# Self-attention on one Trainium2 core: for some query tiles the row maximum is taken from a key-half difference, rectified on ScalarE, with one VectorE pass

## What is computed

```
qkv = h @ w_qkv + b_qkv
q, k, v = jnp.split(qkv, 3, axis=-1)          # 16 heads of 16 features
scores = jnp.einsum('bqhd,bkhd->bhqk', q, k) / np.sqrt(DK)
attn = jax.nn.softmax(scores, axis=-1)
o = jnp.einsum('bhqk,bkhd->bqhd', attn, v)
```

## Time and profile before

| What | Value |
|---|---|
| median of three runs | 2838.29 us |
| profiled execution, first to last instruction (its span) | 2841.2 us |
| projection stage, first bias operation to the first value addition | 616.2 to 660.7 us |
| value tiles, to the next stage | 660.7 to 674.4 us |
| first passes of pairs 0 and 1, alone | 682.6 to 729.2 us, granted clock 0.50 |
| loop with interleaved first pass, 14 pairs | 729.3 to 1134 us, granted clock 1.00 from 758 us on |
| last two pairs | 1134 to 1174 us |
| reductions of the first pass (L1762) | 512, of 682 ns each on the mean |
| exponentials (L1740) | 256, of 1021 ns |

### The profile page before, as it was taken

One profiled execution on the slowest core, in us unless ns is written; L12 is line 12 of the kernel. 1 busy time (PEld: TensorE's weight loads), 2 busy tenths in 40 slices (PEclk: granted clock), 3 DMA queues, 4 the chain that ended last, 5 costly groups with the idle time before them and its releaser, 6 DMA issues. The chain is left out here.

```text
span 2841.2 us, 39450 instructions
## 1 busy us (share of the span) xinstructions
PE 2161.8 (76%) x11928; PEld 1566.3 (55%) x11929; DVE 1271.6 (45%) x2848; ACT 819.6 (29%) x1698; POOL 438.1 (15%) x362
## 2 busy tenths in 40 slices
PE   5587988836899999722999953599999984794298
PEld 4346674622222222321899943488888884584297
DVE  3874672186877777222323343222222222673222
ACT  1120342110355555400333320133333331341021
POOL 0000000000000000005122200444444441000312
PEclk8698998977799999955999965699999997896599
DMA  2001210013001010063122216222222222007121
GB/s 94 32 1 41 66 57 27 4 52 84 23 24 35 24 35 13 13 232 105 32 32 35 31 37 238 71 55 48 50 55 50 49 39 65 3 1 266 52 33 27
DMA packets 128952, 158.27 MB, mean 56 GB/s; under 512 B 24266, under 2 KB 108499, under 8 KB 128693
## 3 DMA queue, kind: packets, MB, share of 16 engines
q1 hardware_dynamic: 100661, 123.14, 14.2%
q0 software_dynamic: 28032, 32.60, 6.6%
HBM read 110.32 MB, written 57.24 MB: 59 GB/s over the span
## 5 line engine op out<-in xcount | busy, mean ns | idle before, releaser
L1377 PE MATMUL banks<-m_rowsT,x_normT 128*128 128x128 f32 x4032 | 491.9, 282 | 51.3 <-DVE m_rowsT L1439 39.1
L1377 PEld LDWEIGHTS banks<-m_rowsT,x_normT 128*128 128x128 f32 x4032 | 474.6, 196 | 87.4 <-issue 79.2
L1387 PE MATMUL banks<-e_w,m_hT 128*128 x2016 | 456.3, 379 | 2.5 <-ACT m_y L1472 2.5
L1387 PEld LDWEIGHTS banks<-e_w,m_hT 128*128 128x128 f32 x2016 | 373.2, 190 | 49.2 <-issue 3.7
L1462 ACT ACTIVATE m_hT<-banks,m_bias 128x128 f32<-128x128 f32 x848 | 241.7, 368 | 414.7 <-PE banks L1377 414.7
L1762 DVE TENSOR_REDUCE sh_mhalf<-banks 128x1 f32<-128x512 f32 x512 | 318.6, 682 | 76.3 <-PE banks L1665 71.7
L1740 ACT ACTIVATE sh_pT<-banks 128x1024 f32<-128x1024 f32 x256 | 249.5, 1021 | 210.5 <-PE banks L1718 210.4
L1334 POOL DMA_INDIRECT scratch_acc<-m_y,m_ids x106 | 181.6, 1713 | 536.5 <-ACT m_y L1472 368.3
L1443 DVE COPY m_ids<-m_rows 128x1 int32<-128x1 int32 x126 | 19.3, 153 | 527.9 <-POOLq L1340 527.9
L1665 PE MATMUL banks<-sh_ks,sh_qs 96*128 96x512 bf16 x512 | 196.1, 416 | 53.6 <-DVE sh_mhalf L1762 33.2
L1424 DVE TENSOR_SCALAR x_normT<-e_w 128x2048 f32 x129 | 160.9, 1248 | 152.7 <-PEq L1393 92.6
(11 more groups left out here) (310 smaller groups left out, 2516.8 us busy)
## 6 DMA issues: line engine op xcount, KB each, us to landing
e_w<-L_W SPq DMA_DIRECT2D x32, 1024.0 KB, 12.9
m_rows<-scratch_rows SPq DMA_DIRECT2D x126, 132.5 KB, 2.2
e_w<-L1f_W SPq DMA_DIRECT2D x16, 1024.0 KB, 12.0
a_bt<-bias SPq DMA_DIRECT2D x16, 616.0 KB, 4.0
scratch_parts<-sp_part SPq DMA_DIRECT2D x48, 128.0 KB, 1.9
sh_qs<-scratch_parts SPq DMA_DIRECT2D x96, 64.0 KB, 2.7
sh_ks<-scratch_parts SPq DMA_DIRECT2D x96, 64.0 KB, 2.8
scratch_acc<-x_resid SPq DMA_DIRECT2D x2, 2048.0 KB, 9.1
```

Source lines behind the costliest of these rows:

```text
L1377: mm = pe.matmul(ps[:, H_BANK + f // 4, f % 4 * P:(f % 4 + 1) * P], w1_tile[:, u, k, f * P:(f + 1) * P], rowsT[:, u, k, :], start=(k == 0) ...
L1387: mm = pe.matmul(ps[:, Y_BANK, 0:D], hT[:, u, f, :], w2_sb[:, bass.ds(e, 1), f, :], start=(f == 0), stop=(f == FB - 1))
```

## The change

For a tile in the new form the maximum over both key halves is computed as the maximum over columns of max(s0, s1) = s1 + relu(s0 - s1). The projection stage computes differences of the key halves, splits them into three bf16 parts, and stores them to a new tensor `scratch_key_steps`. The stack load gets a third kind of transfer (`kd`). In such a tile the first product (bank 0) uses `kd` and gives the difference; ScalarE rectifies it into `rise`; the second product (bank 1) gives the scores of the second half; and VectorE adds `rise` and takes the row maximum with one `tensor_tensor_reduce`. Tiles 1, 4, 7, 9, 12 and 15 of pairs 2 to 15 have this form, and all 16 tiles of pairs 0 and 1. The maxima are now split behind the transpose, so `turn_maxima` has one transpose, `join_maxima` one operation and `maxima_rows` four. The turn of pair 0's maxima is moved behind four chunks of pair 1.

```diff
+RISING_PAIRS = (1, 4, 7, 9, 12, 15)
...
+                    if j >= 2 and c % 2:
+                        m = (n - NQ // 2) // 2
+                        sp.wait_ge(d_split, m + 1)
+                        for i in range(PARTS):
+                            sp.dma_start(parts_d[i, (j % 2) * P:(j % 2 + 1) * P, c // 2 * CH:(c // 2 + 1) * CH], part_d[i][:, m % 2, :]).then_inc(d_stored[m % 2], 16)
...
+                    sp.wait_ge(d_stored[u], 2 * 48)
...
                     if n >= 2:
...
+                    if n > NQ // 2 and n % 2 == 0:
+                        act.wait_ge(d_taken, (n - NQ // 2) // 2)
...
+                    if n >= NQ // 2 and u:
+                        m = (n - NQ // 2) // 2
+                        v = m % 2
+                        dve.tensor_tensor(d32[:], q32[:, 0, :], q32[:, 1, :], ALU.subtract).then_inc(d_taken, 1)
+                        dve.wait_ge(d_taken, m + 1)
+                        if m >= 2:
+                            dve.wait_ge(d_stored[v], 48)
+                        link(dve.tensor_copy(part_d[0][:, v, :], d32[:]))
+                        link(dve.tensor_tensor(d32[:], d32[:], part_d[0][:, v, :], ALU.subtract))
+                        link(dve.tensor_copy(part_d[1][:, v, :], d32[:]))
+                        dve.tensor_tensor(part_d[2][:, v, :], d32[:], part_d[1][:, v, :], ALU.subtract).then_inc(d_split, 1)
...
+            for s in range(NP):
+                for pair in range(2 * KT):
...
                     for j, (i, k) in enumerate(PROD):
+                        sp.dma_start(kd[u][j * DK:(j + 1) * DK, :, :], steps(k)).then_inc(stack_in[u], 16)
...
-                    pe.wait_ge(stack_in[u], 16 * 2 * len(PROD) * (s // U + 1))
+                    pe.wait_ge(stack_in[u], 16 * 3 * len(PROD) * (s // U + 1))
                 if n >= 2:
-                    pe.wait_ge(a_max, n - 1)
-                pe.matmul(ps[:, A_BANK + n % 2, :], qs[u][0:SR, h, t * P:(t + 1) * P], ks[u][0:SR, h, half * CH:(half + 1) * CH],
-                          start=True, stop=True).then_inc(a_mm, 1)
+                    if half == 0 and (c - 2) % NA // 2 in RISING[(n - 2) // NA]:
+                        pe.wait_ge(a_rise, rise_count[n - 1])
+                    else:
+                        pe.wait_ge(a_max, max_count[n - 1])
+                keys = kd[u][:, h, :] if half == 0 and c // 2 in RISING[s] else ks[u][0:SR, h, half * CH:(half + 1) * CH]
+                pe.matmul(ps[:, A_BANK + n % 2, :], qs[u][0:SR, h, t * P:(t + 1) * P], keys, start=True, stop=True).then_inc(a_mm, 1)
...
-                    for i in range(PARTS):
-                        mm = pe.transpose(ps[0:2 * KT, T_BANK, i * P:(i + 1) * P], mpart[i][:], core.ident[:])
-                    mm.then_inc(mT_mm, 1)
+                    pe.transpose(ps[0:2 * KT, T_BANK, 0:P], m32[:], core.ident[:]).then_inc(mT_mm, 1)
...
                 for c in range(NA):
                     first_pass(pe, 0, c)
+                for c in range(4):
+                    first_pass(pe, 1, c)
...
-                for c in range(NA):
+                for c in range(4, NA):
                     first_pass(pe, 1, c)
...
+                def rises(s, pair):
+                    if pair not in RISING[s]:
+                        return
+                    n = s * NA + 2 * pair
+                    i = rise_count[n]
+                    act.wait_ge(a_mm, n + 1)
+                    if i >= 2:
+                        act.wait_ge(a_max, max_at[i - 2])
+                    act.activation(rise[:, i % 2, :], ps[:, A_BANK, :], ACT.Relu).then_inc(a_rise, 1)
...
+                for s in range(2):
+                    for pair in range(2 * KT):
+                        rises(s, pair)
...
+                        if s + 2 < NP:
+                            rises(s + 2, n % (2 * KT))
                         act.wait_ge(b_mm, n + 1)
...
-                        dve.wait_ge(a_mm, n + 1)
-                        dve.tensor_reduce(mhalf[:, half, h * KT + t:h * KT + t + 1], ps[:, A_BANK + n % 2, :], AX, ALU.max).then_inc(a_max, 1)
-                def split_maxima(s):
-                    dve.wait_ge(a_max, (s + 1) * NA)
-                    link(dve.tensor_tensor(m32[:], mhalf[:, 0, :], mhalf[:, 1, :], ALU.max))
-                    link(dve.tensor_scalar(m32[:], m32[:], -1.0, None, ALU.mult))
-                    link(dve.tensor_copy(mbf[0][:], m32[:]))
-                    link(dve.tensor_copy(mpart[0][:], mbf[0][:]))
-                    link(dve.tensor_tensor(m32[:], m32[:], mpart[0][:], ALU.subtract))
-                    link(dve.tensor_copy(mbf[1][:], m32[:]))
-                    link(dve.tensor_copy(mpart[1][:], mbf[1][:]))
-                    dve.tensor_tensor(mpart[2][:], m32[:], mpart[1][:], ALU.subtract).then_inc(m_split, 1)
...
+                        if c // 2 not in RISING[s]:
+                            dve.wait_ge(a_mm, n + 1)
+                            dve.tensor_reduce(mhalf[:, s % 2, half, col:col + 1], ps[:, A_BANK + half, :], AX, ALU.max).then_inc(a_max, 1)
+                        elif half:
+                            dve.wait_ge(a_mm, n + 1)
+                            dve.wait_ge(a_rise, rise_count[n])
+                            dve.tensor_tensor_reduce(larger[:], ps[:, A_BANK + 1, :], rise[:, (rise_count[n] - 1) % 2, :], 1.0, -3e38,
+                                                     ALU.add, ALU.max, mhalf[:, s % 2, 0, col:col + 1]).then_inc(a_max, 1)
...
+                    dve.wait_ge(a_max, max_count[(s + 1) * NA])
+                    dve.tensor_tensor(m32[:], mhalf[:, s % 2, 0, :], mhalf[:, s % 2, 1, :], ALU.max).then_inc(m_split, 1)
...
                 def maxima_rows(s):
...
-                    dve.tensor_copy(mT[:], ps[0:2 * KT, T_BANK, 0:PARTS * P].rearrange("p (i n) -> p i n", n=P)).then_inc(mT_sb, 1)
+                    top = ps[0:2 * KT, T_BANK, 0:P]
+                    link(dve.tensor_scalar(mT[:, 0, :], top, -1.0, None, ALU.mult))
+                    link(dve.scalar_tensor_tensor(mrest[:], top, -1.0, mT[:, 0, :], ALU.mult, ALU.subtract))
+                    link(dve.tensor_copy(mT[:, 1, :], mrest[:]))
+                    dve.tensor_tensor(mT[:, 2, :], mrest[:], mT[:, 1, :], ALU.subtract).then_inc(mT_sb, 1)
...
+                link(dve.memset(mhalf[:], -3e38))
...
-                split_maxima(0)
+                join_maxima(0)
+                reduce_scores(1, range(0, 6))
...
-                reduce_scores(1, range(NA))
-                split_maxima(1)
+                reduce_scores(1, range(6, NA))
+                join_maxima(1)
...
                         reduce_scores(s + 2, range(12, NA))
-                        split_maxima(s + 2)
+                        join_maxima(s + 2)
...
```

More of the change, by code:

```diff
@@ L1610, in self_attention @@
             ks = [sb3(f"ks{u}", [SR + PARTS, 2, SEQ], BF16) for u in range(U)]
[L1611 to L1614 removed]
+            kd = [sb3(f"kd{u}", [SR, 2, CH], BF16) for u in range(U)]
+            rise, larger = sb3("rise", [P, 2, CH]), sb3("larger", [P, CH])
+            mhalf, m32 = sb3("mhalf", [P, 2, 2, 2 * KT]), sb3("m32", [P, 2 * KT])
+            mT, mrest = sb3("mT", [2 * KT, PARTS, P], BF16), sb3("mrest", [2 * KT, P])
             pT = sb3("pT", [P, 4, 2, CH])
@@ L1623, in self_attention @@
             NA = 2 * KT * 2
+            RISING = tuple(RISING_PAIRS if s >= 2 else range(2 * KT) for s in range(NP))
+            rise_count, max_count = [0], [0]
+            for s in range(NP):
+                for pair in range(2 * KT):
+                    rising = pair in RISING[s]
+                    rise_count += [rise_count[-1] + rising] * 2
+                    max_count += [max_count[-1] + (not rising), max_count[-1] + (not rising) + 1]
             @block.sync
@@ L1734, in _ @@
             def _(act):
+                def rises(s, pair):
[7 more added lines that the diff above has]
+                    act.activation(rise[:, i % 2, :], ps[:, A_BANK, :], ACT.Relu).then_inc(a_rise, 1)
+                max_at = [max_count[s * NA + 2 * pair + 2] for s in range(NP) for pair in range(2 * KT) if pair in RISING[s]]
+                for s in range(2):
+                    for pair in range(2 * KT):
+                        rises(s, pair)
                 for s in range(NP):
                     for n in range(s * 2 * KT, (s + 1) * 2 * KT):
+                        if s + 2 < NP:
+                            rises(s + 2, n % (2 * KT))
                         act.wait_ge(b_mm, n + 1)
```

12 lines of the change are left out of this document (8 added, 4 removed).

## The result

The changed kernel takes 2855.74 us (median of 4 runs, 2850.61 to 2858.44), the kernel before 2837.09 us beside it (4 runs, 2834.23 to 2839.83). The ratio is **1.0053, 95% interval 1.0036 to 1.0070**: slower by 15 us (10 to 20). The profiled execution took 2858.4 us with a span of 2856.6 us; the one of before had 2841.2.

What follows compares the result with a forecast made beforehand. It took the loop to be bound by latency from a chunk's product to a free bank, not VectorE's total; 9.1 + 2.8 + 3.2 - 2.4 - 1.0 + 6.9 - 0.2 = +18.4 us gave 2857 us, range 2846 to 2871.

Steps and rivals of the forecast that it cites:

- Projection: Projection stage: four key-difference splits of 2.98 us each on VectorE delay the first value addition by 9.1 us.
- Stack loads: Start of attention: 18 instead of 12 loads per head pair delay the first chunk once, by 2.8 us.
- First two pairs: First two head pairs, all 32 tiles new-form: 1.49 instead of 1.39 us per tile, +3.2 us in all.
- the rival of 2896 us: Rival: the fused VectorE pass runs at half rate, +0.53 us each, total about 2896 us; chance 0.07.
- Turns, -2.4 and -1.0: Maxima handling between the first two head pairs and at loop entry: fewer small operations save 2.4 and 1.0 us.
- Loop, +0.50 a pair: The 14 loop head pairs with six new-form tiles each: +0.50 us per pair, +6.9 us in all.
- k = 2 and 6: Key steps (of 0 to 7) with the new-form tile in the first half-step: later fourth chunk, +0.16 us each.
- k = 7: Last key step: the last exponential stands behind a rectification and delays the second weighted group, +0.23 us.
- k = 0 and 1 together with the transposes: First two key steps, VectorE nearly full: +0.17 us; one transpose instead of three: -0.22 us.
- The cover of the four operations: Key step 2: the four maxima operations end before the tile's rectification, so cost nothing; uncovered they would cost 0.55 us.
- VectorE's total: Rival: VectorE's total work sets the loop, so fewer reductions make the kernel faster, 2816 us; chance 0.06.
- ScalarE's queue as the bound of most steps: Rival: all six late exponentials in a head pair hold TensorE, +16 us, 2873 us; chance 0.07.

Runs made afterwards that it cites:

- the experiment with the differences alone: Kernel before with the new handling of the maxima, plus difference splits and stores that nothing loads or uses, old tiles; 2839.67 us, run once.
- The kernel with the new maxima alone: Kernel before with only the new handling of the maxima, no differences, third transfer or new-form tiles; 2831.82 against 2833.65 us, ratio 0.9993.
- the filler: Kernel before plus 56 unused 128x512 VectorE reductions behind the last reduction of key steps 3 to 6; 2831.83 against 2833.65 us, ratio 0.9991.

## Why the prediction was right, and which of its terms were not

Forecast 2857 us, +18.4; measured 2855.7, +15.0 by the ratio. The sign, the mechanism and the two largest places were as argued, but the sum had 6 us more than the +12.1 that the stage itself became longer. That 2857 lies so near 2855.7 is therefore partly luck: in the profiled execution 4.3 us more passed behind the stage, of which the sum knew nothing.

1. **Projection, +9.1.** Right: +9.09. The five operations take 646.41 - 643.43 = 2.98 us, and the store waits behind the key chunks are gone.
2. **Stack loads, +2.8.** From SP's first load to the first chunk 693.29 - 683.12 = 10.17 us, before 682.55 - 674.43 = 8.12: +2.05 (the experiment with the differences alone gives 1.8). The rate of issue was right; the last transfer landed sooner after its issue (2.2 us against 2.9). With 0.6 us among the value tiles, which I had not seen coming, the stretch comes to +2.67. SP's first load in the kernel before:

```profile
674.43 0.33 SPq L1633 DMA_DIRECT2D sh_qs<-scratch_parts  x1
```

3. **First two pairs, 1.49 us a tile, +3.2.** The mis-sized term. A tile takes 696.10 - 694.70 = 1.40 us. I took 0.80 for the fused operation and its accumulator write, and it was the low end of my range: the write (83 ns) starts 0.62 us after a pass of 0.69 us and lies in the overlap; the next instruction of VectorE starts 0.62 us after the fused one in step 2 (921.97), and the bank is taken again after 0.76 us (922.11), as after a plain reduction (928.30 to 929.05). So the fused operation costs what a reduction does, and the part is +0.2 instead of +3.2. The Trainium skill, "Vector Engine (DVE) Microarchitecture Reference", section "Points that are easy to get wrong", has its half rate for two SBUF sources that are not bf16. Here one of the two is in PSUM, and 692 ns for 512 columns is the time of a pass at full rate: the rival of 2896 us is refuted. Whether the page's sentence covers this operation, which the trace calls CUSTOM_DVE_ANT_0, no run here shows. The upper end of this part was also added up wrongly: 0.87 us for both gives 32 x 0.17 = +5.4, not +5.8.
4. **Turns, -2.4 and -1.0.** The first is -2.54, right. The second was -2.41. The kernel with the new maxima alone has -2.25, so the gain is theirs. The first of the 14 loop pairs lies in this stretch too, so without the 0.4 us that it became longer the turn gained about 2.8. I had counted the small operations only. Behind them TensorE works without the gap, and the granted clock rises sooner: from the first step's first product at 738.13 in after it is full in the stretch from 743, while before, with the first product at 729.65, it was still 0.50 up to 739 and 0.86 in the four us after (from 743 on it is full there too, not only from 758, as the table of times has it). The windows of both kernels, before first:

```profile
735.00:739.00 4.00, 4.00 (x14) 0.67 (x13) 2.58 (x4) 2.05 (x2) 0.00 (x0) 0.50 0.00 0
739.00:743.00 4.00, 3.66 (x23) 1.26 (x19) 2.68 (x5) 1.94 (x2) 0.00 (x0) 0.86 0.02 5
```

```profile
739.00:743.00 4.00, 4.00 (x11) 1.17 (x10) 2.34 (x8) 2.96 (x5) 0.00 (x0) 0.56 0.00 0
743.00:747.00 4.00, 3.79 (x20) 1.04 (x19) 3.42 (x8) 2.23 (x3) 0.00 (x0) 1.00 0.00 0
```

   That the removed gap is what lets the clock rise is argued from these rows, not shown apart from the gap itself. The one table load of the stage, whose move I had not considered, now stands at this place (738.0 us, 1.28 us long; in the kernel before at 674.4) and ends as the first exponential starts, at 739.3; no run here separates its price.

5. **Loop, +0.50 a pair.** +0.40. (The ends of this part, +1.8 and +14.7, were given without their working.) The single steps: k = 3 and 4, predicted 0, measured 0 (3.54 and 3.51 us as before). k = 2 and 6, predicted +0.16 each, measured +0.14 and +0.15. That is two errors which cancel: the fused operation is shorter than I took (0.69, not 0.80), but the hand-over from the rectification takes 921.35 - 921.21 = 0.14 us where I took 0.03. k = 7, predicted +0.23, measured +0.22: the 16 weighted products that close the pair take 2.13 us instead of 1.91, the second group behind the exponential, just as argued.

```profile
940.65 2.13 PE L1746 MATMUL banks<-sh_pT,sa_vh 128*17 128x512 f32 x16
...
941.73 0.13 PEld L1746 LDWEIGHTS banks<-sh_pT,sa_vh 128*17 128x17 f32 x8 [0.94 <-ACT sh_pT L1794]
```

   k = 0 and 1 together with the transposes, predicted -0.05, measured about -0.12 (6.14 against 6.26 us), since tile 1 costs 0.1 and not 0.17. The cover of the four operations held, and the experiments price it at 0.41 us a pair.

The rivals: VectorE's total (0.06) is refuted by the filler and by the change itself; the half rate by 692 ns; ScalarE's queue as the bound of most steps by steps 3 and 4, which did not move with a late exponential (in step 7 alone one holds TensorE, as forecast).

The prediction did not name where the gain was to be had. Its chain for step 4 began with "product 0.44" ahead of the first chunk, and it treated that as given; it was a link that could be moved.

## What to carry over

Before relieving an engine, write down the chain of one loop iteration with its links and look whether the engine's idle time is in it: here 1.03 us of idle in every 3.51 us step said that VectorE's total did not matter, and only a shorter latency or another order could. When a chain goes out to another engine and back, put independent work of the first engine inside the round trip, not ahead of it: moving two chunks ahead of two products saved 0.43 us in each plain step, without a single instruction less. And small operations are free or not by what stands beside them, so an experiment that removes a tile also removes a cover.

## What the runs showed of the hardware

- A VectorE pass that adds two operands (one in PSUM, one in SBUF, both 128x512 f32) and keeps the running maximum takes 692 ns, as long as a 128x512 subtraction with both operands in SBUF (0.69 us) and, by the means, 7 ns more than a plain maximum over one (691 against 684). The accumulator write behind it takes 83 ns and adds nothing, as it lies in the overlap with the pass. On ScalarE the accumulator read takes 187 ns.
- The hand-over from the end of a rectification on ScalarE to the start of the fused operation on VectorE was 0.14 us (0.14 to 0.18 in the 85 cases in which VectorE waited for it); TensorE's next product starts 0.06 us after the fused operation's write ends (922.05 to 922.11).
- A rectification of 128x512 from PSUM takes 597 ns on ScalarE, 12 more than the copy of the earlier trace rows, and between exponentials it brought no second table load.
- At TensorE's lower clock two products of a step in a row take 1.06 us instead of 0.60. If an idle stretch ahead of the loop keeps the granted clock low for longer, as the rows of the turns (4. above) suggest but do not prove, it is paid twice: once itself, and again in the steps until the clock is back at full.
